# Small-head attentions: weighed values on four column tiles, and the values formed just ahead of them

## The reference, cut to what matters

```
q, k, v = x @ Wq.T + bq, ctx @ Wk.T + bk, ctx @ Wv.T + bv      # 16 heads of 8
scores  = q k^T / sqrt(8)  (+ causal mask, or + a window and a top-64 choice)
attn    = softmax(scores)
out     = (attn @ v) @ Wo.T + bo
```

## Time and profile before

| | us |
|---|---|
| time, median of 3 runs | 872.35 |
| lowest and highest | 871.7 and 872.58 |
| span of the profiled execution, first to last instruction | 868.2 |
| median less span (start and end around the instructions) | 4.15 |
| second attention, weighed values of tile 0 to tile 13 | 634.0 to 699.7 |
| third attention with the last feed-forwards | about 745 to 868 |

### The profile page before, as it was taken

One profiled execution on the slowest core, in us unless ns is written; L12 is line 12 of the kernel. 1 busy time (PEld: TensorE's weight loads), 2 busy tenths in 40 slices (PEclk: granted clock), 3 DMA queues, 4 the chain that ended last, 5 costly groups with the idle time before them and its releaser, 6 DMA issues.

```text
span 868.2 us, 18067 instructions
## 1 busy us (share of the span) xinstructions
PE 835.6 (96%) x6180; PEld 579.6 (67%) x6180; DVE 632.4 (73%) x1587; ACT 566.6 (65%) x1569; POOL 286.3 (33%) x586
## 2 busy tenths in 40 slices
PE   9999999999999999999999999999999989899996
PEld 8887888888889976644444443444477765677662
DVE  5677776777776655675784866765989867888876
ACT  3666677677776676776545476455467779677664
POOL 4355444444554442210000000002146630334455
PEclk9999999999999999999999999999999999999999
DMA  8600000000000000000000000000000000000000
GB/s 342 154 2 2 1 2 1 2 2 1 2 1 2 2 1 2 1 1 0 1 0 1 0 1 0 1 0 1 1 27 3 2 3 1 2 2 3 2 14 37
DMA packets 7813, 13.42 MB, mean 15 GB/s; under 512 B 4342, under 2 KB 5036, under 8 KB 7468
## 3 DMA queue, kind: packets, MB, share of 16 engines
q1 hardware_dynamic: 7724, 12.27, 4.5%
HBM read 11.22 MB, written 1.05 MB: 14 GB/s over the span
## 4 chain that ended last, share of the span: by engine, by line
PE 61%; DVE 18%; POOL 10%; issue 5%; ACT 4%; DMA 0%; DVEq 0%; POOLq 0%; SPq 0%; ACTq 0%
PE psum L1551 10%; PE psum L767 6%; PE psum L807 4%; POOL rstd L515 4%; PE psum L750 3%; PE psum L759 3%; POOL arena L1095 2%; DVE negmax L1005 2%; PE psum L1996 2%; PE psum L835 2%; DVE arena L2082 2%; PE psum L1978 2%; PE psum L1560 2%; ACT arena L905 2%; PE psum L2489 2%
## 5 line engine op out<-in xcount | busy, mean ns | idle before, releaser
L512 POOL TENSOR_TENSOR ve<-mv,epsv 128x1 f32<-128x1 f32 x176 | 36.3, 206 | 460.3 <-DVE mv L507 460.3
L1551 PE MATMUL psum<-arena,w1f 128*128 128x512 f32 x240 | 110.0, 594 | 0.0
L515 POOL TENSOR_TENSOR rstd<-ve,epsv 128x1 f32<-128x1 f32 x176 | 101.2, 575 | 13.8
L905 ACT ACTIVATE arena<-psum,negmax 128x128 f32<-128x128 f32 x256 | 90.3, 406 | 22.2 <-DVE negmax L1005 22.2
L1551 PEld LDWEIGHTS psum<-arena,w1f 128*128 128x128 f32 x240 | 45.9, 191 | 50.3 <-issue 46.4
L1095 POOL TENSOR_TENSOR arena<-arena,rsum 128x512 f32<-128x512 f32 x64 | 65.2, 1039 | 5.6 <-DVE rsum L1011 5.6
L1005 DVE TENSOR_REDUCE negmax<-psum 128x8 f32<-128x1024 f32 x32 | 39.2, 1224 | 32.9 <-PE psum L807 32.9
L905 ACT ACTIVATION_READ_ACCUMULATOR arena<-psum,negmax 128x1 f32 x256 | 63.0, 246 | 0.0
L750 PE MATMUL psum<-arena,sclA 128*128 128x128 f32 x512 | 62.5, 275 | 0.1
L767 PE MATMUL psum<-arena 128*128 128x512 f32 x128 | 61.2, 598 | 0.7 <-DVE arena L1000 0.4
L521 DVE TENSOR_SCALAR yln<-x_tok,mv,rstd 128x128 f32<-128x128 f32 x128 | 53.4, 429 | 9.3 <-POOL rstd L515 8.0
(11 more groups left out here) (371 smaller groups left out, 2012.5 us busy)
## 6 DMA issues: line engine op xcount, KB each, us to landing
w<-in_w0qk SPq DMA_DIRECT2D x2, 512.0 KB, 4.8
w<-in_w0vo SPq DMA_DIRECT2D x1, 1024.0 KB, 7.4
cT<-in_cT SPq DMA_DIRECT2D x1, 1024.0 KB, 16.5
out<-x_tok SPq DMA_DIRECT2D x4, 256.0 KB, 2.0
rows<-in_rows SPq DMA_DIRECT2D x1, 836.0 KB, 12.3
x_tok<-in_x_tok SPq DMA_DIRECT2D x1, 768.0 KB, 9.5
ctx_tok<-in_ctx_tok SPq DMA_DIRECT2D x1, 768.0 KB, 10.8
wa<-in_wa SPq DMA_DIRECT2D x1, 768.0 KB, 18.1
```

What stands on the lines that cost most here:

```text
L515: pool.tensor_tensor(rstd[:, u, self.i:self.i + 1], ve[:, u, self.i:self.i + 1], epsv[:, 1:2], ALU.pow) \
L905: m = nc.scalar.activation(e0[:, b, g, :], ps(k, P, j * P), ACT.Exp, bias=negmax0[:, b, g:g + 1], accum_out=sum0[:, b, g:g + 1])
L1551: nc.tensor.matmul(ps(k), w1("e2", j * 384 + arg * D, j * 384 + (arg + 1) * D), f1_Hm[:, n, 2 * j + i, :], start=False, stop=False)
```

## The change

Three edits. The weighed values are formed for 32 queries at a time: 32 products of 32 stationary columns a tile in both attentions, in turn on the four column tiles of 32. The values of the second attention are formed for 32 tokens at a time: 8 products of 32 stationary columns. And in the lists of the second attention, `v` moves on TensorE from behind `lnt` to behind `out`, straight ahead of `av`, and on ScalarE from ahead of `ot` to behind `t`. Banks, lags, the written lists of start and drain, `form_values` and the lists of the third attention stay.

```diff
--- before.py
+++ after.py
@@ -1292,8 +1292,8 @@
         END_BANKS = {("ha1", PREV): 7, ("f21", PREV): 4, ("hh1", LAST): 5, ("f110", LAST): 6, ("f111", LAST): 7, ("ha1", LAST): 5,
                      ("f21", LAST): 6, ("xo", PREV): 4, ("xo", LAST): 4}
         ATT_BANKS = {"s0": 0, "s1": 1, "s2": 2, "s3": 3, "lnt": 4, "v": 6, "ot": 7, "t1": 5, "t0": 4, "out": 7, "av": 6, "qk": 7, "lnt0": 5}
-        ATT_PE = [("s", 4), ("lnt", 9), ("v", 5), ("ot", 7), ("t", 5), ("out", 7), ("av", 6), ("qk", 2), ("lnt0", 1)]
-        ATT_ACT = [("lnt", 9), ("v", 5), ("ot", 7), ("t", 5), ("qk", 2), ("lnt0", 1), ("s", 4)]
+        ATT_PE = [("s", 4), ("lnt", 9), ("ot", 7), ("t", 5), ("out", 7), ("v", 5), ("av", 6), ("qk", 2), ("lnt0", 1)]
+        ATT_ACT = [("lnt", 9), ("ot", 7), ("t", 5), ("v", 5), ("qk", 2), ("lnt0", 1), ("s", 4)]
         ATT_DVE = [("own", 0), ("max", 4), ("tail", 8), ("add", 7), ("s", 4), ("rsum", 6), ("stats", 7), ("av", 6), ("apply", 0)]
         ATT_POOL = [("root", 0), ("km", 2), ("tail", 7), ("bias", 8), ("own", 1)]
         ATT_LAST = 9
@@ -1958,10 +1958,10 @@
                     k = a.bank("v", t)
                     fill(pe, a, "v", t)
                     for b in range(2):
-                        for r in range(2):
-                            w = wgt(n, "v").rearrange("p (g q c) -> p g q c", q=2, c=DH2)[:, :, r, :]
-                            m = nc.tensor.matmul(psum[r * S:(r + 1) * S, k, b * S:(b + 1) * S], cT[:, t.n * P + b * S:t.n * P + (b + 1) * S],
-                                                 w, start=True, stop=True)
+                        for i in range(4):
+                            w = wgt(n, "v").rearrange("p (g q c) -> p g q c", q=2, c=DH2)[:, :, i // 2, :]
+                            x = t.n * P + b * S + i % 2 * 32
+                            m = nc.tensor.matmul(psum[i * 32:(i + 1) * 32, k, b * S:(b + 1) * S], cT[:, x:x + 32], w, start=True, stop=True)
                     m.then_inc(full[k], 1)
                 if kind == "ot":
                     k = a.bank("ot", t)
@@ -1993,8 +1993,9 @@
                         stored(pe, a, f"t{i}", t)
                     for g in range(HALF):
                         for b in range(2):
-                            m = nc.tensor.matmul(psum[b * S:(b + 1) * S, k, g * 18:(g + 1) * 18], pT2[:, u, g, b * S:(b + 1) * S],
-                                                 Vx[:, u, b * HALF + g, :], start=True, stop=True)
+                            for q in (slice(b * S, b * S + 32), slice(b * S + 32, (b + 1) * S)):
+                                m = nc.tensor.matmul(psum[q, k, g * 18:(g + 1) * 18], pT2[:, u, g, q], Vx[:, u, b * HALF + g, :],
+                                                     start=True, stop=True)
                     m.then_inc(full[k], 1)
                 if kind == "qk":
                     k = a.bank("qk", t)
```

## The result

| us | before | changed |
|---|---|---|
| median of 12 runs each, on the same chips | 871.65 | 873.45 |
| lowest and highest | 870.26 and 873.49 | 872.75 and 875.91 |
| profiled execution: time | not recorded | 873.56 |
| profiled execution: span | 868.2 | 871.7 |

The changed kernel takes 1.0028 times the time of the one before (95% interval 1.0018 to 1.0038). The forecast was 877.5. The sign is right, the time lies in the range, but the loss is 1.8 us in the medians where 5.15 was forecast. A second build of the same pair gave 874.62 against 871.45, 1.0033 [1.0016, 1.005], a loss of 3.2.

The account below looks back on a forecast made before the run. With no engine having much room, it took the order of one step in the second attention as the bound. 868.2 + 8.0 - 0.8 - 2.5 + 0.5 = 873.4 us span, 877.5 us time; range 869 to 889.

Parts of the forecast that it names:

- the hole: Second attention: TensorE idle for 0.74 us between v and av, until ScalarE's copies free bank 6.
- the ring: Second attention, exp to next exp through TensorE and ScalarE: 5.67 us instead of 5.06, 13 steps, +8.0 us.
- the drain: End of the second attention: av of tiles 14 and 15 counted in full, 2 x 0.41, -0.8 us.
- the third attention: Chain of waits passes through av six times from 782.68 to 828.50: six times 0.41, -2.5 us; bounds 0 to -6.6.
- the instructions: 2,304 more instructions, nine more fetches on the instruction queue: +0.5 us; bounds 0 to 3.
- av to qk: Weighed values per tile: from 1.05 to 0.64 us if four column tiles run together; bounds 0.64, 1.05, 1.98.
- The base: Profiled span of 868.2 us plus 4.15 around it, up to the median of 872.35, left unchanged.
- the hole lowers the clock: Sign of being wrong: a lower granted clock from TensorE's idle time before av; no size given.
- 1 (all of the third attention's gain): Rival: VectorE has slack in the third attention, all 16 av count, 873.4 us; chance 0.12.
- 2: Rival: only two column tiles run at once, av keeps 1.05, ring 6.31, 889 us; chance 0.14.
- 3 (29 ns a pass): Rival: 29 ns a pass stays, av 1.98, ring 7.24, about 918 us; chance 0.05.
- 4: Rival: the hole doesn't open, second attention stays at VectorE's pace near 5.0, 869 us; chance 0.15.

Follow-up runs that it names:

- order alone: Kernel before with only v moved on TensorE and ScalarE, products of 64 as before: 880.9 us against 871.57, 1.0113.
- blocks alone: Changed kernel with the old order of v on TensorE and ScalarE, so only the 32-column products remain: 867.45 us, 0.9952 of the kernel before.
- bank 5: Changed kernel with v of tiles 2 to 14 in bank 5 instead of 6: 867.35 us, 0.9953; with dummy products in the third attention added, 866.78 us, 0.9958.
- two tiles: Changed kernel with av's two loops exchanged, so successive products use only two of four column tiles: one run, 881.25 us.
- the wide products: Changed kernel with v in bank 5, and 64-column products for v of tile 15 and av of tiles 14 and 15 in the second attention: 867.18 us, 0.9958.
- blocks for av alone: Kernel before with av in blocks of 32 queries in both attentions, v and order as before: median 868.76 us, 0.9973.
- the two repeats: Changed kernel run twice more with nothing changed: 1.0033 of the kernel before, and 873.21 us once.
- the blocks there alone: Kernel before with blocks of 32 queries in the third attention alone: 870.32 us against 870.64, 0.999.

## What the prediction had right, and which steps failed

The mechanism of the loss was right: the shared bank, the hole of 0.69 for 0.74, and who ends it. Four terms of the sum failed in size, and they nearly cancel: the ring +8.0 (measured +5.5), the drain -0.8 (+0.1 to +0.3), the third attention -2.5 (-1.2 to -1.3), and the instructions +0.5 (no such time found). Together they made +5.2 where the profiles show 4.3 to 4.8. That this sum came close is luck. The rest of the miss, down to 1.8 between the medians, is a term that the sum did not have, the half-clock stretches, and a base put together from two executions; both are treated below.

**The ring: the mechanism right, the size 2.5 us too large.** Predicted +8.0, measured 71.20 - 65.73 = +5.5, the low bound as stated (13 steps of 0.61 - 0.2 make 5.3). The step was forecast at 5.67 and is 5.58: out to v is 0.31 where I took the 0.39 of out to av, t to out 0.93 where I took 0.97, and av to qk 0.67 where I took 0.64. That is 0.09 a step, 0.9 us over ten steps. The larger miss is the count. "13 steps ... have a v just ahead" is true, but only eleven go the whole ring: the intervals of av are 5.73, ten of 5.58, then 5.41 and 4.24. Jobs that run ahead of v end first: lnt0 is done with tile 15 one step before qk, so that ScalarE's exp no longer stands behind its copy (5.41), and then qk with its copies is gone (4.24). By my sum the last two would have been 5.67 each: 1.7 more than they were. I counted the waits, and not the edges that make each wait cost a full step.

**What the blocks are worth.** av to qk fell from 1.05 to 0.67, against 0.64 predicted. The order alone gives steps of 5.95, with blocks 5.58: the 0.37 is cashed in full where the ring sets the pace. Without the hole only 0.13 of it is. Of the rest, 1.7 us in 50, or 0.17 a step, is the wait for VectorE shown above.

**The drain.** Predicted -0.8, measured +0.34, and +0.07 and +0.06 in two other profiles. The term took for granted that nothing else would take the time that the shorter av left. The first av did save its 0.38 (1.79 for 2.17); the pause inside v of tile 15 ate that and more (4.46 for 3.74). It was 0.86, 0.59 and 0.59 in three profiles of the changed kernel, 0.40 with blocks alone, 0.67 and 0.41 in two with bank 5, 0.26 with two tiles, and is absent with the wide products. In these seven it stands before the same instruction of TensorE, counted from the kernel's start with the weight loads; with blocks for av alone it stands exactly 256 instructions earlier in the count. 256 is also what one fetch brings: the change has 2,304 instructions and 9 fetches more (51 to 60). The same code pausing for different times at a place bound to the instruction count, with nothing that the profile shows to wait for, fits a late instruction fetch. Why only this fetch is late, of those in the stage, no run shows, so the cause stays argued, though strongly. The place where it hurt was not among my bounds.

**The instructions.** The +0.5 rests on a misreading of the earlier trace rows. The 12 gaps of "issue" before av are gaps of the weight loader, counted with TensorE's; TensorE alone has none before av, neither in the kernel before nor in the changed one. Nor do they follow the fetches: 3.9 us with 51 and 4.5 with 60 in this pair, but 4.6 with 51 (the order alone) and 3.7 with 60 (blocks alone). The fetches rose by nine as forecast, and the only time found with them is the pause above.

**The third attention.** "Six times 0.41: -2.5" is wrong by half: -1.16 in the profile, -1.28 and -1.22 in the two repeats, -1.27 with the blocks there alone. I took every passage of the chain through av for a saving. Of a second profile of the changed kernel, the chain of waits from 745 to 870 keeps these:

```profile
754.69 0.67 PE psum L1997 x50
...
793.77 0.67 PE psum L1997 x51
...
819.66 0.67 PE psum L1997 x50
...
826.18 0.82 PE psum L1997 x53
...
831.84 0.67 PE psum L1997 x50
```

In the kernel before the chain goes through av of tiles 0, 1, 6, 7, 8, 11, 12 and 13; here through 0, 7, 11, 12 and 13 (in the other two profiles through 8 too). The av of tile 1 and of tile 6 (755.20 and 782.68 in the earlier trace rows) are off it: once av is shorter, another chain ends last there. By intervals of av, -0.39 fell in the first five steps, of which I expected nothing, -0.33 in the next three, +0.10 in two, and -0.66 in the last five. Between 750 and 776 TensorE gained idle time: 0.7 and 0.6 us of it end with VectorE, 0.7 with ScalarE's store of a transposed tile.

**The base.** I put the change on top of 872.35. "4.15 lie around it ... and I leave those" joins an execution to the median of others. The executions of which time and span are both known have 1.8 between them (873.56 and 871.7; 870.01 and 868.2). So the profiled one before took about 870.0, and it held a half-clock stretch at 354.0 that cost 1.4 us (634.01 against 632.59), which the one after did not; its start is 1.2 shorter. My span of 873.4 was 1.7 above the 871.7 measured: ring -2.5, start -1.2, instructions -0.5, against drain +1.1, third attention +1.3, end +0.1. The other 2.3 of the miss of 4.05 is the difference between 4.15 and 1.86.

**What the change is worth, like with like.** From av of tile 0 to the end the three profiles of the changed kernel are 4.8, 4.3 and 4.5 us longer than the first of the kernel before. Executions with the same mean granted clock of 0.999, though not on the same chip: 868.76 and 869.02 before, 872.85 to 873.09 in four of the changed kernel, +4.1. On the chip of the repeats the shared means are lower and the answer is wider: 872.2 to 873.6 against 877.7 at 0.993, 875.2 against 876.8 at 0.991. The medians say 1.8 and 3.2. Executions of the kernel before had more stretches at half clock: most of its means lay between 0.993 and 0.997, those of the changed one between 0.996 and 0.999. One such stretch more in an execution, at the 1.4 us that it cost at 354 and at 747, is of the size of the difference, but no run takes them away, so this part is argued. Why the kernel before has more is open. That the hole lowers the clock, which I had named as a way to be wrong, did not come: the granted clock from 634 to 700 us is 1.00 with the hole.

**The rivals.** 1 (all of the third attention's gain) is out: -1.3. Its time of 873.4 came true, for another reason. 2 is out by av's 0.74 and by the two-tile run. 3 (29 ns a pass) is out: (0.74 - 0.18) / 63 = 9 ns between starts on average, over 64 passes in turn on four column tiles. The Trainium skill ("TensorE: Matmul & The Clock Gate", section "Wait — 56ns, not 53.3ns?") has starts never closer than about 25 ns; for passes on different tiles this trace does not agree, and the measurement decides. 4 is out for this kernel, and it is what the bank-5 version does: the hole doesn't open, and the time is 867.35, better than the 869 I gave it.

**Which version to keep.** Blocks without the hole: 867.35 with v in bank 5, 867.45 with the old order. Both are 0.5% faster than the kernel before. No run tells them apart by time.

## What to carry to other kernels

Before a producer is moved next to its consumer, list the buffers of both: two fills of one bank back to back make the second wait for the reader of the first, which here made the second 0.82 us later in every step, while another bank gave the same order for nothing. Price a new wait by the full ring it closes, and count only the steps in which every edge of the ring exists, so not the last ones of a pipeline. A chain of waits gives the most that a shorter operation can save; here the next chain allowed half of it. Look at which engine a gap belongs to before you price it. And a difference of a few tenths of a per cent is read stage by stage, between profiles with and without stretches at half clock, and not from two medians.

## What the hardware showed that I had not expected

- Sixty-four float32 passes of 32 stationary columns on four column tiles start 9 ns apart on average: 16 rounds of 35 ns. On two tiles the same passes take 32 rounds of 29 ns (1.10 us), and the old 64-column passes 16 rounds of 58 ns (1.11 us). Half the columns on two tiles gains nothing; four tiles together do.
- A run of small products can stop in the middle of one tile's work for 0.3 to 0.9 us with no wait in the profile. The place kept to TensorE's instruction count and moved by 256 instructions, one fetch, when the code ahead changed; wide products there made the pause go.
- The granted clock fell to 0.5 for about 3.4 us at places that differ between executions of one program: for the kernel before at 354 us in one profile, at 747 in another, at 783 and 841 in a third, which also has one of 10.3 us at 18.5. The changed kernel has one at 782 in two profiles and none before the last microseconds in the third. In its first profile TensorE stood idle for 0.23 and 0.81 us before the fall:

```profile
780.05 0.33 PE L634 MATMUL psum<-const,yln 128*128 128x128 f32 x1 [0.23 <-ACT lnT L644]
...
781.19 0.68 PE L266 MATMUL psum<-const 128*128 128x128 f32 x4 [0.81 <-DVE x_tok L573]
```

```profile
782.00:788.00 6.00, 6.00 (x81) 4.66 (x82) 4.96 (x25) 2.41 (x7) 1.58 (x4) 0.72 0.00 0
```

  The profile without a fall has the same two pauses there (0.22 and 0.81), so they alone don't decide it. A fall of 3.4 us cost from 0.1 us (at 782, where the stage was hardly longer) to 1.7 us (at 841), by the stage times of profiles with and without it.
